# Routed experts' loop: both sets of transposes ahead of the up and down products

## The chip, the core and the metric

The kernel runs on one core of a Trainium2 chip. The metric is the device time of one execution in microseconds (us). Before the change it is 2602.16 us, the median of 3 runs (2601.45 to 2602.78).

## The reference

Two layers of a graph network, each followed by experts. The change touches only the last block, the routed experts (64 experts, 2 per row, 3125 rows of 512 numbers), in which every expert computes, for the rows that were sent to it:

```python
h = silu(buf @ w1[e]) * (buf @ w3[e])     # 512 -> 256
y = h @ w2[e]                             # 256 -> 512
...
return x + shared + routed
```

All of it is float32.

## The kernel before

Stages run one after the other: the attention graph layer, its experts, a normalization, the second graph layer with its gate, and then `phase_moe`, which the profile shows from about 1850 us to the end. In `phase_moe` a first half of the shared expert's products runs beside the routing. Then comes the routed experts' loop (about 1996 to 2446 us), and after it the second half of the shared expert, gathers of the experts' results, and the final sums.

The loop works on items. An item is up to 128 rows of one expert; the trace has 72 of them. Each item needs, by engine:

- POOL gathers its 128 rows (`mo_g`, 256 KB) by an indirect DMA (L2115).
- TensorE (PE) transposes them, four 128x128 blocks (L2218, semaphore `turned`), and ScalarE (ACT) copies the result from PSUM to `mo_xT` (L2265, `cop`).
- PE makes the up products, `mo_xT` by `w13`: 4 calls, 8 instructions of 128x512 in the trace (L2203, `up`).
- ACT takes the sigmoid of one half (L2253, `sgd`), and VectorE (DVE) multiplies twice (L2425, L2427) into `mo_hh` (`hd`).
- PE transposes `mo_hh`, two blocks (L2212, `ht`); ACT copies them to `mo_hT` (L2259, `hc`).
- PE makes the down products, `mo_hT` by `w2`: 2 calls, 4 instructions in the trace (L2225, `yd`); DVE copies the result to `mo_y` (L2433, `yc`); ACT issues the store to `ys` (L2269).
- SP loads each expert's weights four items ahead: `w1` and `w3` (L2063, 512 KB each, into `w13`) when the up products of the item four before are done, and `w2` (L2068, 512 KB) when its down products are. SP issues in order: up load of n, down load of n, up load of n+1.

The items are pipelined by hand. Each engine runs the function `step(n)` in program order; PE's step n works on items n-1 (up), n-2 (transposes of `hh`), n (transposes of the gathered rows) and n-2 again (down). Eight steps are written out, then a loop `Fori` runs bodies of four steps, and the last steps are written out again. No scheduler moves anything: the order in the source is the order on each engine, and only waits on semaphores tie the engines together. The buffers `eX`, `eH`, `eU`, `eY`, `xT`, `sg`, `hh` and `hT` are double.

Of the kernel before, what the change touches and what calls it, by code (L numbers as in the profile page):

```python
# [8 lines left out]
ACT = mybir.ActivationFunctionType  # L9
# [7 lines left out]
P = 128  # L17
N = 3125
D = 512
KT = D // P  # L20
# [19 lines left out]
E1, F1, TOP, CAP1 = 64, 256, 2, 1024  # L40
# [49 lines left out]
def wait(eng, sem, value):  # L90

    if not isinstance(value, int) or value > 0:
        eng.wait_ge(sem, value)
# [1813 lines left out]
FT = F1 // P  # L1907


def phase_moe(nc, K, a, xmid, tab3, xsh, ys, xnT, s13, s2, top, tix, out):  # L1910
# [13 lines left out]
    with Phase(nc, "mo") as p:  # L1924
# [12 lines left out]
        eX, eH, eU, eY = psA, psB, psY, psR  # L1937
# [34 lines left out]
        g = p.sb("g", [P, NW, D])  # L1972
        w2 = p.sb("w2", [P, NW, FT, D])
        xT = p.sb("xT", [P, 2, KT, P])
        sg = p.sb("sg", [P, 2, F1])
        hh = p.sb("hh", [P, 2, F1])
# [34 lines left out]
        turned = p.sem("turned")  # L2011
# [21 lines left out]
        def prev(n, k, q, j):  # L2033

            return n - j, k + (q - j) // NW, (q - j) % NW

        def n_ok(n, q, j):


            if ended[0]:  # L2040
                return q < j
            return not isinstance(n, int) or n >= j
# [111 lines left out]
        @b.tensor  # L2154
        def _(t):
            tens = nc.tensor

            def ranks():
                t.wait_ge(bothd, 1)
                for c in range(CH):  # L2160
                    wait(t, taken, c - 1)
                    cols = both[:, c * TC:(c + 1) * TC, :].rearrange("p t e -> p (t e)")
                    o = (psR, psY)[c % 2]
                    tens.matmul(o[0][:, 0:TC * E1], tri16[:, 0, :], cols, start=True, stop=True)
                    tens.matmul(o[1][:, 0:TC * E1], tri16[:, 1, :], cols, start=True, stop=True).then_inc(ranked, 1)

            def overs():
                t.wait_ge(oqd, 1)
                tens.matmul(psR[1][0:1, 0:P], oq[:], K.ident[:], start=True, stop=True).then_inc(ovd, 1)

            def slots(r):
                t.wait_ge(od, r + 1)
                for i in range(PB):
                    ins = tens.matmul(psR[0][0:NI1, 0:2 * P], oa[:, i, :], ob[:, i, 1:3].rearrange("p w b -> p (w b)"),  # L2174
                                      start=(r == 0 and i == 0), stop=(r == CH - 1 and i == PB - 1), skip_group_check=True)
                ins.then_inc(om, 1)

            def turn():
                t.wait_ge(idd, 1)
                tens.transpose(psR[1][:, 0:NI1], idf[:], K.ident[0:NI1, 0:NI1]).then_inc(idt, 1)  # L2180

            after = {1: ranks, 3: overs, 6: lambda: slots(0), 7: lambda: slots(1), 8: lambda: slots(2),
                     9: lambda: slots(3), 10: lambda: slots(4), 11: turn}
            for j in range(G1):
                for f in range(KT):
                    shared_up(t, j, f)
                    if f == 0 and j:
                        shared_down(t, j - 1)
                    after.get(j * KT + f, lambda: None)()
            shared_down(t, G1 - 1)  # L2190
            t.wait_ge(routed, 1)
            t.wait_ge(zd, NSH)

            def step(n, k, q):
                u = q % 2
                m, km, qm = prev(n, k, q, 1)
                if n_ok(n, q, 1):
                    um = qm % 2
                    t.wait_ge(cop, m + 1)
                    t.wait_ge(wl[qm], km * 32 + 32)  # L2200
                    wait(t, hd, m - 1)
                    for kt in range(KT):
                        ins = tens.matmul(eH[um][:], xT[:, um, kt, :], w13[:, qm, kt, :],  # L2203
                                          start=(kt == 0), stop=(kt == KT - 1))
                    ins.then_inc(up, 1)
                m, km, qm = prev(n, k, q, 2)
                um = qm % 2
                if n_ok(n, q, 2):
                    t.wait_ge(hd, m + 1)
                    wait(t, hc, m - 1)  # L2210
                    for c in range(FT):
                        ins = tens.transpose(eU[um][:, c * P:(c + 1) * P], hh[:, um, c * P:(c + 1) * P], K.ident[:])  # L2212
                    ins.then_inc(ht, 1)
                if n_ok(n, q, 0):
                    t.wait_ge(got[q], k * 16 + 16)
                    wait(t, cop, n - 1)
                    for kt in range(KT):
                        ins = tens.transpose(eX[u][:, kt * P:(kt + 1) * P], g[:, q, kt * P:(kt + 1) * P], K.ident[:])  # L2218
                    ins.then_inc(turned, 1)
                if n_ok(n, q, 2):  # L2220
                    t.wait_ge(hc, m + 1)
                    t.wait_ge(vl[qm], km * 16 + 16)
                    wait(t, yc, m - 1)
                    for c in range(FT):
                        ins = tens.matmul(eY[um][:], hT[:, um, c, :], w2[:, qm, c, :], start=(c == 0), stop=(c == FT - 1))  # L2225
                    ins.then_inc(yd, 1)
            run(t, 2, step)

            for j in range(G1, len(groups)):
                for f in range(KT):  # L2230
                    shared_up(t, j, f)
                    if f == 0 and j > G1:
                        shared_down(t, j - 1)
            shared_down(t, len(groups) - 1)

        @b.scalar
        def _(c_):
# [7 lines left out]
            c_.wait_ge(routed, 1)  # L2245

            def step(n, k, q):
                m, km, qm = prev(n, k, q, 1)
                um = qm % 2
                if n_ok(n, q, 1):  # L2250
                    c_.wait_ge(up, m + 1)

                    nc.scalar.activation(sg[:, um, :], eH[um][:, 0:F1], ACT.Sigmoid).then_inc(sgd, 1)  # L2253
                m, km, qm = prev(n, k, q, 2)
                um = qm % 2
                if n_ok(n, q, 2):
                    c_.wait_ge(ht, m + 1)
                    wait(c_, yd, m - 1)
                    nc.scalar.activation(hT[:, um], eU[um][:, 0:F1].rearrange("p (c t) -> p c t", t=P),  # L2259
                                         ACT.Copy).then_inc(hc, 1)  # L2260
                if n_ok(n, q, 0):
                    u = q % 2
                    c_.wait_ge(turned, n + 1)
                    wait(c_, up, n - 1)
                    nc.scalar.activation(xT[:, u], eX[u][:].rearrange("p (k t) -> p k t", k=KT), ACT.Copy).then_inc(cop, 1)  # L2265
                m, km, qm = prev(n, k, q, 3)
                if n_ok(n, q, 3):
                    c_.wait_ge(yc, m + 1)
                    c_.dma_start(ys[ds(m * P, P), :], y[:, qm, :]).then_inc(st[qm], 16)  # L2269
# [216 lines left out]
```

## Time and profile before

| | |
|---|---|
| median of 3 runs | 2602.16 us |
| the profiled execution's own time | 2601.69 us |
| its span on the core | 2599.8 us |
| PE busy in the span | 2092.5 us (80%) |
| DVE busy | 1466.5 us (56%) |
| POOL busy | 1019.4 us (39%) |
| ACT busy | 658.1 us (25%) |
| mean rate of the DMA engines | 222 GB/s |

A busy share is an average over all stages. What a change in one stage is worth is read from the timeline and the waits of that stage: an engine that is idle for a short time in each turn of a loop pays for it as many times as the loop turns. Matmul durations overlap, so the time that one matmul costs is the distance to the start of the next, and not the duration that its row shows.

### The profile page before, as it was taken

The page shows a single profiled execution, that of the slowest core. Times are in us where ns is not written, and L with a number is a line of the kernel's source. Part 1 is how long each engine was busy: PE and PEld are TensorE (multiplying, and loading weights), DVE is VectorE, ACT ScalarE, POOL GpSimd, SP SyncE. Part 2 cuts the span into 40 slices and gives each one's busy share as a digit, 9 for nine tenths or more (in the row PEclk, how much of TensorE's full clock was granted, in tenths as well). Part 3 has the DMA queues.
Part 4 walks back from the last instruction along what each step waited for, and adds up shares of the span by engine and source line. Part 5 has one row for each costly group of instructions (what it writes and reads, how often), then busy time and mean ns, then how long its engine had stood idle before and what let it go on. Part 6 is the DMA issues. An engine that isn't in the chain of part 4 may idle for free. (4 is left out here: it accounts for less than half of the span.)

```text
span 2599.8 us, 30846 instructions
## 1 busy us (share of the span) xinstructions
PE 2092.5 (80%) x7552; PEld 1232.3 (47%) x7552; DVE 1466.5 (56%) x3483; ACT 658.1 (25%) x2048; POOL 1019.4 (39%) x1082
## 2 busy tenths in 40 slices
PE   3864888888886615339999977789899999999998
PEld 2653666666665614214444422245544444444444
DVE  5447989989998672265554544467673222222243
ACT  1223655655554301320000000034200121212100
POOL 1017777777750003347777777600001111111241
PEclk9887999999997556769999999999799999999999
DMA  5978888888854533687777777686314999999662
GB/s 158 287 286 260 252 250 242 249 239 242 241 165 134 169 97 69 127 278 230 230 233 230 214 210 210 200 293 227 126 46 139 336 340 335 339 338 335 209 232 95
DMA packets 284539, 577.81 MB, mean 222 GB/s; under 512 B 46565, under 2 KB 124613, under 8 KB 281673
## 3 DMA queue, kind: packets, MB, share of 16 engines
q0 software_dynamic: 87136, 303.18, 38.9%
q1 hardware_dynamic: 175827, 234.11, 27.6%
q10 hardware_dynamic: 21462, 39.19, 4.1%
q8 instruction: 47, 0.77, 0.1%
q14 instruction: 67, 0.55, 0.1%
HBM read 476.16 MB, written 101.00 MB: 222 GB/s over the span
## 5 line engine op out<-in xcount | busy, mean ns | idle before, releaser
L801 PE MATMUL g_psA<-g_G,g_oh 128*128 128x261 f32 x1760 | 434.2, 398 | 94.8 <-DVE acc L969 52.3
L1098 PE MATMUL g_psA<-g_G,g_oh 128*128 128x512 f32 x880 | 408.3, 602 | 121.3 <-DVE g_oh L1129 77.2
L1063 POOL DMA_INDIRECT g_G<-tab,src_of_item x440 | 416.6, 947 | 183.7 <-issue 175.5
L741 POOL DMA_INDIRECT g_G<-tab,src_of_item x440 | 419.7, 954 | 157.2 <-issue 104.2
L801 PEld LDWEIGHTS g_psA<-g_G,g_oh 128*128 128x128 f32 x1760 | 328.4, 194 | 165.6 <-DVE g_G L951 97.6
L1098 PEld LDWEIGHTS g_psA<-g_G,g_oh 128*128 128x128 f32 x880 | 159.3, 191 | 348.2 <-issue 339.8
L856 ACT ACTIVATE g_G<-g_G 128x64 f32<-128x64 f32 x1320 | 317.8, 338 | 0.0
L1138 DVE TENSOR_TENSOR acc<-acc,g_psA 128x512 f32 x220 | 151.3, 688 | 282.1 <-PE g_psA L1098 278.8
L2115 POOL DMA_INDIRECT mo_g<-tab,mo_slot x72 | 68.0, 945 | 490.5 <-PE mo_bank L2218 361.4
L2203 PE MATMUL mo_bank<-mo_w,mo_xT 128*128 128x512 f32 x576 | 259.1, 592 | 1.4 <-ACT mo_xT L2265 1.4
L951 DVE TENSOR_TENSOR g_G<-g_G,g_psP 128x640 f32<-128x640 f32 x220 | 179.1, 814 | 5.3 <-ACT g_G L847 5.3
L2139 PE MATMUL mo_bank<-own,s 128*128 128x512 f32 (+1 forms) x448 | 178.1, 556 | 4.3 <-DVE mo_shT L2293 3.1
L2203 PEld LDWEIGHTS mo_bank<-mo_w,mo_xT 128*128 128x128 f32 x576 | 109.3, 190 | 138.7 <-issue 136.8
L969 DVE TENSOR_TENSOR acc<-acc,g_psA 128x522 f32 x220 | 152.6, 693 | 32.0 <-PE g_psA L801 30.7
L2425 DVE TENSOR_TENSOR mo_sg<-mo_sg,mo_bank 128x256 f32<-128x256 f32 x72 | 30.3, 421 | 228.2 <-ACT mo_sg L2253 228.2
L2225 PE MATMUL mo_bank<-mo_w,mo_hT 128*128 128x512 f32 x288 | 142.3, 617 | 11.1 <-ACT mo_hT L2259 6.0
L2139 PEld LDWEIGHTS mo_bank<-own,s 128*128 128x128 f32 x448 | 81.1, 193 | 96.5 <-issue 92.4
L2253 ACT ACTIVATE mo_sg<-mo_bank 128x256 f32<-128x256 f32 x72 | 27.6, 384 | 354.4 <-PE mo_bank L2203 354.4
L1129 DVE TENSOR_SCALAR g_oh<-iota,rel_of_item 128x128 f32<-128x128 f32 x440 | 113.3, 310 | 0.0
L2433 DVE COPY mo_y<-mo_bank 128x512 f32<-128x512 f32 x72 | 49.8, 692 | 108.8 <-PE mo_bank L2225 108.8
L2150 PE MATMUL mo_bank<-s,mo_shT 128*128 128x512 f32 x200 | 89.6, 605 | 9.6 <-DVE mo_shT L2293 3.4
L2130 POOL DMA_INDIRECT own<-ys,mo_pair x50 | 51.0, 1020 | 113.0 <-DVE own L2452 56.5
(382 smaller groups left out, 2635.5 us busy)
## 6 DMA issues: line engine op xcount, KB each, us to landing
mo_w<-in_L_ffn_w SPq DMA_DIRECT2D x216, 512.0 KB, 5.7
ys<-mo_y ACTq DMA_DIRECT2D x72, 256.0 KB, 4.4
fi_rl<-reld POOLq DMA_DIRECT2D x10, 1408.0 KB, 14.5
oht<-fi_oo POOLq DMA_DIRECT2D x10, 1408.0 KB, 10.7
g_G<-tab,src_of_item POOLq DMA_INDIRECT x880, 3.7
g_ot<-oht SPq DMA_DIRECT2D x26, 512.0 KB, 5.5
ys<-sg_zeros SPq DMA_DIRECT2D x24, 512.0 KB, 3.9
g_pen<-pend SPq DMA_DIRECT2D x208, 32.0 KB
```

The source lines that it names most:

```text
L741: q.indirect_dma_start(G[:, j % RING, :], None, tab0, bass.IndirectOffsetOnAxis(K.src[:, j:j + 1], 0)).then_inc(gs[g % 3], 16)
L801: ins = tens.matmul(psA[u][:, f, 0:HW], oh[:, n % OR, h, :], G[:, r + h, f * HW:(f + 1) * HW], start=(h == 0), stop=(h == SUP - 1))
L856: ins = sc.activation(x, x, ACT.Copy, scale=G[:, r, hd * HC + HD:(hd + 1) * HC])
L951: vv.tensor_tensor(x, x, w.unsqueeze(3).to_broadcast([P, SUP, HV, HD]), ALU.mult).then_inc(ready, 1)
L969: vv.tensor_tensor(a1, a1, psA[u][:, :, 0:HW], ALU.add).then_inc(added, 1)
L1063: g.indirect_dma_start(G[:, q, h, :], None, table, bass.IndirectOffsetOnAxis(K.src[:, j:j + 1], 0)).then_inc(got[q], 16)
L1098: ins = nc.tensor.matmul(psA[u][:], oh[:, q % OB, h, :], G[:, q, h, 0:D], start=(h == 0), stop=(h == SUP - 1))
L1129: ins = vv.tensor_scalar(oh[:, q % OB, h, :], K.iota[:], K.rel[:, ds(n * SUP + h, 1)], None, ALU.is_equal)
L1138: ins = vv.tensor_tensor(a1, a1, psA[u][:], ALU.add)
L2139: ins = nc.tensor.matmul(o[c % 2][:, 0:w_], s13[:, i, kt, f * P:(f + 1) * P], xnT[:, tiles[0]:tiles[-1] + 1, kt * P:(kt + 1) * P], start=( ...
L2203: ins = tens.matmul(eH[um][:], xT[:, um, kt, :], w13[:, qm, kt, :], start=(kt == 0), stop=(kt == KT - 1))
L2225: ins = tens.matmul(eY[um][:], hT[:, um, c, :], w2[:, qm, c, :], start=(c == 0), stop=(c == FT - 1))
```

## The change

On PE, step n now begins with the transposes of the gathered rows of item n, then those of `hh` of item n-2; after them the up products of item n-1 and the down products of item n-2. On ACT, the step's order becomes: copy of `xT` for item n, copy of `hT` for item n-2, sigmoid for item n-1, store of item n-3. SP, POOL and DVE keep their programs. No instruction that computes is added or removed, and every wait stands before the same work as before.

```diff
 # PE
             def step(n, k, q):
                 u = q % 2
+                if n_ok(n, q, 0):
+                    t.wait_ge(got[q], k * 16 + 16)
+                    wait(t, cop, n - 1)
+                    for kt in range(KT):
+                        ins = tens.transpose(eX[u][:, kt * P:(kt + 1) * P], g[:, q, kt * P:(kt + 1) * P], K.ident[:])
+                    ins.then_inc(turned, 1)
+                m, km, qm = prev(n, k, q, 2)
+                um = qm % 2
+                if n_ok(n, q, 2):
+                    t.wait_ge(hd, m + 1)
+                    wait(t, hc, m - 1)
+                    for c in range(FT):
+                        ins = tens.transpose(eU[um][:, c * P:(c + 1) * P], hh[:, um, c * P:(c + 1) * P], K.ident[:])
+                    ins.then_inc(ht, 1)
                 m, km, qm = prev(n, k, q, 1)
                 if n_ok(n, q, 1):
...
                 if n_ok(n, q, 2):
-                    t.wait_ge(hd, m + 1)
...
-                    ins.then_inc(ht, 1)
-                if n_ok(n, q, 0):
-                    t.wait_ge(got[q], k * 16 + 16)
...
-                    ins.then_inc(turned, 1)
-                if n_ok(n, q, 2):
                     t.wait_ge(hc, m + 1)
 # ACT
-                if n_ok(n, q, 1):
-                    c_.wait_ge(up, m + 1)
-
-                    nc.scalar.activation(sg[:, um, :], eH[um][:, 0:F1], ACT.Sigmoid).then_inc(sgd, 1)
+                if n_ok(n, q, 0):
+                    u = q % 2
+                    c_.wait_ge(turned, n + 1)
+                    wait(c_, up, n - 1)
+                    nc.scalar.activation(xT[:, u], eX[u][:].rearrange("p (k t) -> p k t", k=KT), ACT.Copy).then_inc(cop, 1)
...
-                if n_ok(n, q, 0):
...
+                if n_ok(n, q, 1):
+                    c_.wait_ge(up, m + 1)
+
+                    nc.scalar.activation(sg[:, um, :], eH[um][:, 0:F1], ACT.Sigmoid).then_inc(sgd, 1)
```

PE, the first of the four steps of the loop's body, before (ISA and REGISTER_ALU rows compute and apply the values of waits; a call of 128x512 is two instructions in the trace):

```order
L2200 ISA
L93 REGISTER_ALU
L2203 MATMUL mo_bank<-mo_w,mo_xT 128x512 x4
L2209 REGISTER_ALU
L93 REGISTER_ALU
L2212 MATMUL mo_bank<-ident,mo_hh 128x128 x2
L2215 ISA
L2218 MATMUL mo_bank<-ident,mo_g 128x128 x4
L2222 ISA
L2225 MATMUL mo_bank<-mo_w,mo_hT 128x512 x2
```

The same step of PE now:

```order
L93 ISA
L2200 MATMUL mo_bank<-ident,mo_g 128x128 x4
L93 REGISTER_ALU
L2208 MATMUL mo_bank<-ident,mo_hh 128x128 x2
L2214 ISA
L93 REGISTER_ALU
L2217 MATMUL mo_bank<-mo_w,mo_xT 128x512 x4
L2224 ISA
L2227 MATMUL mo_bank<-mo_w,mo_hT 128x512 x2
```

The six transposes stood between the up and the down products; they now stand between the down products of one step and the up products of the next. Between the transposes of `hh` and the down products that use them, there were four transposes; there are now the four calls of the up products too.

ACT, the second step of the body, before (the bank is that of the PSUM buffer read):

```order
L2253 ACTIVATE mo_sg<-mo_bank2 128x256
L2259 ACTIVATE mo_hT<-mo_bank5 128x256
L2263 REGISTER_ALU
L2265 ACTIVATE mo_xT<-mo_bank1 128x512
L2269 ISA
L2269 DMA ys<-mo_y 128x512
```

ACT, the same step now:

```order
L2252 REGISTER_ALU
L2254 ACTIVATE mo_xT<-mo_bank1 128x512
L2260 ACTIVATE mo_hT<-mo_bank5 128x256
L2267 ACTIVATE mo_sg<-mo_bank2 128x256
L2271 ISA
L2271 DMA ys<-mo_y 128x512
```

The sigmoid went from the first place to the third, and the copy of `xT` from the third to the first; the store's issue stays last.

## Rows read from the trace of the kernel before

**Rows 1.** Page, section 4: the chain that ended last, by line.

```profile
PE mo_bank L2203 10%; PE mo_bank L2225 5%; PE mo_bank L2139 5%; PE mo_bank L2150 3%; ACT mo_hT L2259 1%; POOL own L2130 1%; DMA own<-ys,mo_pair 0%; PE mo_bank L2174 0%; DVE mo_ssg L2289 0%; DVE mo_shT L2293 0%; PE mo_bank L2212 0%; DVE mo_prd L2354 0%; DVE mo_ovb L2355 0%; DVE mo_pos L2353 0%; DVE mo_prd L2352 0%
```

**Rows 2.** Waits from 2026 to 2436 us: in total, times, longest.

```profile
PEld mo_bank L2225 <- issue: 39.7, 148, 0.5
PEld mo_bank L2225 <- ACT mo_hT L2259: 16.6, 50, 0.3
PE mo_bank L2225 <- ACT mo_hT L2259: 4.8, 16, 0.3
```

**Rows 3.** Timeline, one period: start us, duration us, engine, line, output, inputs, count, [idle].

```profile
2206.65 3.60 PE L2203 MATMUL mo_bank<-mo_w,mo_xT 128*128 128x512 f32 x8
2210.08 0.38 PE L2212 MATMUL mo_bank<-ident,mo_hh 128*128 128x128 f32 x2
2210.28 0.39 ACT L2253 ACTIVATE mo_sg<-mo_bank 128x256 f32<-128x256 f32 x1 [4.91 <-PE mo_bank L2203]
2210.30 0.60 PE L2218 MATMUL mo_bank<-ident,mo_g 128*128 128x128 f32 x4
2210.56 0.38 ACT L2259 ACTIVATE mo_hT<-mo_bank 128x256 f32<-128x256 f32 x1
2210.70 0.42 DVE L2425 TENSOR_TENSOR mo_sg<-mo_sg,mo_bank 128x256 f32<-128x256 f32 x1 [3.06 <-ACT mo_sg L2253]
2210.94 0.60 ACT L2265 ACTIVATE mo_xT<-mo_bank 128x512 f32<-128x512 f32 x1
2210.99 0.30 PEld L2225 LDWEIGHTS mo_bank<-mo_w,mo_hT 128*128 128x128 f32 x2 [0.33 <-ACT mo_hT L2259]
2211.16 0.42 DVE L2427 TENSOR_TENSOR mo_hh<-mo_sg,mo_bank 128x256 f32<-128x256 f32 x1
...
2212.82 3.60 PE L2203 MATMUL mo_bank<-mo_w,mo_xT 128*128 128x512 f32 x8
```

**Rows 4.** The same timeline, the down products of the next step, first of a body.

```profile
2217.37 1.96 PE L2225 MATMUL mo_bank<-mo_w,mo_hT 128*128 128x512 f32 x4 [0.30 <-ACT mo_hT L2259]
```

**Rows 5.** Timeline of PE in the second graph layer's gate stage, straight code.

```profile
1744.81 0.61 PE L1829 MATMUL sg_psT<-ident,sg_ag 128*128 128x128 f32 x4
1745.26 3.60 PE L1836 MATMUL sg_psH<-sg_w,sg_xT 128*128 128x512 f32 x8
1748.69 0.60 PE L1843 MATMUL sg_psN<-ident,sg_xn 128*128 128x128 f32 x4
1749.13 1.00 PE L1819 MATMUL sg_psG<-sg_gT,own 128*128 128x64 f32 x8
```

**Rows 6.** Timeline of PE: up products of item 2, of item 71, and what follows.

```profile
2008.08 3.60 PE L2203 MATMUL mo_bank<-mo_w,mo_xT 128*128 128x512 f32 x8
...
2436.41 3.60 PE L2203 MATMUL mo_bank<-mo_w,mo_xT 128*128 128x512 f32 x8
...
2442.75 0.38 PE L2212 MATMUL mo_bank<-ident,mo_hh 128*128 128x128 f32 x2
```

**Rows 7.** Stretches: length, busy of PE, PEld, DVE, ACT, POOL; PE clock, DMA share, GB/s.

```profile
2000.00:2006.00 6.00, 5.31 (x20) 2.66 (x18) 0.88 (x3) 1.43 (x4) 0.94 (x1) 1.00 1.05 390
2100.00:2200.00 100.00, 97.67 (x290) 46.85 (x290) 24.54 (x48) 20.04 (x48) 15.52 (x17) 1.00 1.00 337
```

**Rows 8.** Page, section 6: DMA issues, count, KB each, us to landing.

```profile
mo_w<-in_L_ffn_w SPq DMA_DIRECT2D x216, 512.0 KB, 5.7
ys<-mo_y ACTq DMA_DIRECT2D x72, 256.0 KB, 4.4
```

**Rows 9.** Timeline of SP: the loads issued after one item's down products.

```profile
2200.68 0.37 SPq L2068 DMA_DIRECT2D mo_w<-in_L_ffn_w  x1
2201.59 0.94 SPq L2063 DMA_DIRECT2D mo_w<-in_L_ffn_w  x2
```

**Rows 10.** Line 2063 from 1990 to 2450 us: issue durations (ns) and landing.

```profile
L2063 SPq DMA_DIRECT2D mo_w<-in_L_ffn_w x136: 372/395/1332, 2000.9 to 2419.9; - x136
...
DMA to landing us min/median/max: 4.3/6.0/9.8
```

More of the change, by code:

```diff
@@ L2207, in step @@
                 um = qm % 2
-                if n_ok(n, q, 2):
-                    t.wait_ge(hd, m + 1)
-                    wait(t, hc, m - 1)
-                    for c in range(FT):
-                        ins = tens.transpose(eU[um][:, c * P:(c + 1) * P], hh[:, um, c * P:(c + 1) * P], K.ident[:])
-                    ins.then_inc(ht, 1)
-                if n_ok(n, q, 0):
-                    t.wait_ge(got[q], k * 16 + 16)
-                    wait(t, cop, n - 1)
-                    for kt in range(KT):
-                        ins = tens.transpose(eX[u][:, kt * P:(kt + 1) * P], g[:, q, kt * P:(kt + 1) * P], K.ident[:])
-                    ins.then_inc(turned, 1)
                 if n_ok(n, q, 2):
@@ L2247, in step @@
             def step(n, k, q):
-                m, km, qm = prev(n, k, q, 1)
-                um = qm % 2
-                if n_ok(n, q, 1):
-                    c_.wait_ge(up, m + 1)
-                    nc.scalar.activation(sg[:, um, :], eH[um][:, 0:F1], ACT.Sigmoid).then_inc(sgd, 1)
+                if n_ok(n, q, 0):
[3 more added lines that the diff above has]
+                    nc.scalar.activation(xT[:, u], eX[u][:].rearrange("p (k t) -> p k t", k=KT), ACT.Copy).then_inc(cop, 1)
                 m, km, qm = prev(n, k, q, 2)
@@ L2260, in step @@
                                          ACT.Copy).then_inc(hc, 1)
-                if n_ok(n, q, 0):
[L2262 to L2265, printed above, removed]
+                m, km, qm = prev(n, k, q, 1)
+                um = qm % 2
+                if n_ok(n, q, 1):
+                    c_.wait_ge(up, m + 1)
+                    nc.scalar.activation(sg[:, um, :], eH[um][:, 0:F1], ACT.Sigmoid).then_inc(sgd, 1)
                 m, km, qm = prev(n, k, q, 3)
```

## The prediction

> **What bounds the kernel now.** I read the chain of waits first: the up products (10% of the span) and the down products (5%) of the routed experts' loop are its two largest pieces, and the copy of `hT` on ACT stands in it with 1% [rows 1]. So TensorE sets the loop's pace, with something small in between. The waits of the loop say what: in 66 steps the down products waited 66 times (50 and 16) for that copy, 21.4 us in all, or 0.32 us each [rows 2]. The timeline of one period shows why: the two transposes of `hh` start at 2210.08, the copy of their result runs from 2210.56 to 2210.94, the four transposes of the gathered rows cover only until about 2210.74 (2210.30 and four distances of 0.11), and the first weight load of the down products comes at 2210.99 [rows 3]. PE is held once in every step by a copy that has only four short transposes to hide behind. In the first step of each loop body the down products start later still, 7.29 us after the mark 2210.08 where the period of 6.17 and the usual 0.91 would make 7.08: some 0.2 us more [rows 3, 4].
>
> **The change, part by part.**
>
> PE's work in a step, without waits: 8 up matmuls take 3.43 us (2206.65 to 2210.08), so 0.43 each, and the 4 down matmuls 1.72. The transposes of `hh` take 0.22 (2210.08 to 2210.30) [rows 3], the other four 0.44, the distance from L1843 to what follows it in the gate stage [rows 5]. Sum: 3.43 + 1.72 + 0.22 + 0.44 = 5.81 us. The loop's real mean is (2436.41 - 2008.08) / 69 = 6.21 us, from item 2's up products to item 71's [rows 6]. The bubble is 0.40 us per step: 0.25 of waiting for ACT, 0.10 for a first weight load that can't start ahead (the up products start at 2212.82, which is 1.83 and not 1.72 after 2210.99) [rows 3], and the 0.2 of one step in four.
>
> *The down products* now have the whole up products between themselves and the transposes they need. The copy of `hT` ends about 0.5 + 0.38 us after those transposes start, behind a copy of `xT` of 0.60 at worst: 1.5 us, against a cover of 3.43 us [rows 3]. The wait goes, and so does the exposed load. In the first step of a body a register computation for the wait on `w2` stood behind the blocked wait for `hT`; nothing blocks there now, so it runs while the up matmuls do. Gain: the whole 0.40.
>
> *What is late next: the transposes of `hh`.* They come first of all that needs the gate, and the up products now queue behind them. The chain to them: up products end at 2210.08, sigmoid at 2210.28, multiplications at 2210.70 and 2211.16, done at 2211.58 [rows 3]: 1.50 us, some 1.55 with the signal. The cover is the down products and four transposes, 1.72 + 0.44 = 2.16 us. A margin of 0.6 us, no wait. ACT has its copies behind it when the sigmoid becomes due (they fall at the step's start), and the store's issue, last on ACT as before, waits for a DVE copy that the down products of the step before released.
>
> *Transposes straight into up products* do not occur in the loop before without a wait. The price lies between 0 and the exposed load of 0.10 per step. The nearest row is the gate stage, the same shapes in the same order with no wait due: four transposes at 1744.81, eight matmuls of 128x512 at 1745.26, 0.45 us where 4 x 0.11 = 0.44 would be [rows 5]. I take 0.01 per step, 1 us in all with what registers add; the end of the range is 0.10, or 6.9 us. I see no reason for a gain below nothing.
>
> *ACT's new order* costs nothing by itself: `xT` is needed a step later (over 5 us for 0.60), `hT` as above. *POOL's gathers* wait for `turned`, still once per step, with four buffers. *SP* is moved past nothing: its loads follow the end of the down and up products at the same places in the step.
>
> *Head.* In the first two steps the up products waited for the copy of `xT` twice; now once, since item 1's copy hides behind item 0's up products. In exchange the first transposes of `hh` wait with no down products as cover: 1.55 - 0.44 = 1.1 us. Saved: 0.9 (0.2 + 0.60 + 0.1 load) and the bubble of 0.35 ahead of item 0's down products. It evens out within 0.2 us; I take 0.
>
> *Tail.* Item 71's up products end at 2439.84 and two transposes at 2440.06, but the next transposes, at 2442.75, put the down products before them at 2442.75 - 1.72 = 2441.03 [rows 6]: a bubble of 1.0 us that goes too. The last item keeps its chain.
>
> Sum: 69 x 0.40 = 27.6, or from the ends 428.3 - 69 x 5.81 = 27.4; + 1.0 tail - 1 for the new transition = 27.4 us. What follows the loop moves with it. The profiled execution took 2601.69 us for a span of 2599.8, so 1.9 lies around it; it becomes 2601.69 - 27.4 = 2574.3. The median of the runs is 0.5 above it: 2574.8, say **2575 us**.
>
> **DMA.** A faster PE asks for more. An item moves three loads of 512 KB, a store of 256 KB [rows 8] and a gather of 128 rows x 512 x 4 bytes: 2.10 MB. In 6.21 us that is 338 GB/s, the 337 of the middle of the loop, at a DMA share of 1.00; in 5.81 us it is 361 GB/s. At the loop's start, with the same kinds of transfer queued, the engines moved 390 GB/s for 6 us [rows 7]. So 361 is within reach, though a share of 1.00 says that not much is left. There is also a store of time: up loads go out at 2201.6 to 2202.5, after the down products that end at about 2200.5 [rows 9], for up products three steps later; 3 x 5.81 + 0.66 - 2.0 = 16 us, less 6.0 to land [rows 10]: 10 us of lead to consume before PE waits at all.
>
> The Trainium skill, in DMA: Bandwidth & Descriptors, section Bandwidth, speaks against this: a load of 1 MB by itself reaches 341 GB/s, and the HBM side is put at about 358 GB/s per core when both of a pair stream. At 341 an item would take 6.15 us and the lead would be gone after some 30 steps: the gain would be 27.4 - (69 x 0.34 - 10) = 14 us, 2588. At 358 it would take 5.86, 3 us in the whole loop, which the lead swallows. The 390 GB/s of the loop's first stretch disagrees with both as a ceiling; the long-run mean here has never been seen above 338.
>
> **Rivals.**
> 1. *DMA becomes the bound.* For it: share 1.00, and issues on SP that last up to 1332 ns instead of 372 [rows 10], as if queues were full. Against it: landing in 6.0 us, under a period, and 390 GB/s. If no more than 338 GB/s can be held, an item takes 6.21: 69 x 0.40 = 27.6 less a lead of 10 is lost, 17.6, so the gain is 10 and the time 2592. If 350 GB/s, the deficit of 0.18 x 69 = 12.6 less 10 costs 3: 2578. It decides below about 352 GB/s. Chance 15%. (The Trainium skill's 341 GB/s, above, would be a case of this one.)
> 2. *The bubble moves instead of going.* The first load of the up products is exposed after the transposes (6.9 us in all) and the register work of the body's first step stays exposed before them (17 x 0.2 = 3.4): 2575 + 9 = 2584. For it: in the loop a load of 0.10 does show. Against it: there it followed a wait; in the gate stage none shows. Chance 12%.
> 3. *Slower: the gate's chain governs.* The transposes of `hh` come before the up products, so a late `hh` now stops all of PE. The chain of 1.55 us has 2.16 of cover; it costs from 2.16 on, and the change loses from 2.16 + 0.40 = 2.56 us. It would take a DVE copy of `y` (0.7 us) plus a store's issue (0.34) both ahead of the gate's work in every step. At 2.7 us the loss is 69 x 0.14 = 10: 2612. The timeline has both well clear of it. Chance 3%.
> 4. *No change*: the wait for `hT` was only the last of several, another 0.3 us behind. The down products' other waits, for `w2` and for `y`, are steps old. Chance 3%.
>
> **How the numbers follow.** Forecast 67%, within 2572 to 2579; rivals 15, 12, 3 and 3%. The range takes in the second rival and most of the first: 2572 to 2588. Faster by over 0.2% (below 2597, about what can be told from no change): 67 + 15 + 12 = 94%, less 1 for what I overlook, 93%. Same 4%, slower 3%.
>
> **What would show it.** In the changed profile, up products should follow each other every 5.81 us, the two transposes of `hh` with no idle before them, the down products with no wait on ACT; the loop's middle should show some 360 GB/s and a clock of 1.00 as now, landing times still near 6 us. Landing times that grow along the loop and waits of PE on DMA in its last third mean rival 1; idle of PEld ahead of the up products means rival 2; idle ahead of the transposes, released by DVE, rival 3.

## The result, and the profile after

The changed kernel takes 2579.44 us (median of 4 runs, 2571.49 to 2585.7); the kernel before, run beside it, 2602.47 (4 runs, 2601.45 to 2608.01). The ratio is 0.9899, 95% interval 0.9876 to 0.9922: 23 us less, where 27 had been forecast. That lies within the stated range of 2572 to 2588 and 0.4 us above the 2572 to 2579 in which the prediction put its own forecast. The profiled execution took 2583.86 us for a span of 2581.8.

The gain is where the prediction put it. Waits of PE (in us, times, longest) from 2012 to 2420 us, in which [rows 2] had 66 waits for the copy of `hT`, 21.4 us in all:

```profile
PEld mo_bank L2217 <- issue: 100.7, 421, 0.2
PEld mo_bank L2227 <- issue: 67.9, 284, 0.2
PEld mo_bank L2200 <- issue: 36.4, 138, 0.3
PEld mo_bank L2208 <- issue: 0.6, 1, 0.6
```

These four are all of PEld's; no row for PE itself and none with ACT, DVE or DMA as releaser is left. The "issue" rows are weight loads that come when their matmul is near, 0.24 us apart from the load before, under a PE that is busy. One period of the timeline (start, duration, engine, line, output, inputs, count, [idle]), to be laid beside [rows 3]:

```profile
2195.01 0.38 PE L2208 MATMUL mo_bank<-ident,mo_hh 128*128 128x128 f32 x2
2195.12 0.30 PEld L2217 LDWEIGHTS mo_bank<-mo_w,mo_xT 128*128 128x128 f32 x2
2195.20 0.60 ACT L2254 ACTIVATE mo_xT<-mo_bank 128x512 f32<-128x512 f32 x1 [1.77 <-PE mo_bank L2200]
2195.22 3.60 PE L2217 MATMUL mo_bank<-mo_w,mo_xT 128*128 128x512 f32 x8
...
2195.70 0.38 ACT L2260 ACTIVATE mo_hT<-mo_bank 128x256 f32<-128x256 f32 x1
...
2198.66 1.88 PE L2227 MATMUL mo_bank<-mo_w,mo_hT 128*128 128x512 f32 x4
...
2198.86 0.38 ACT L2267 ACTIVATE mo_sg<-mo_bank 128x256 f32<-128x256 f32 x1 [2.78 <-PE mo_bank L2217]
...
2199.28 0.42 DVE L2427 TENSOR_TENSOR mo_sg<-mo_sg,mo_bank 128x256 f32<-128x256 f32 x1 [3.81 <-ACT mo_sg L2267]
...
2199.73 0.42 DVE L2429 TENSOR_TENSOR mo_hh<-mo_sg,mo_bank 128x256 f32<-128x256 f32 x1
...
2200.38 0.60 PE L2200 MATMUL mo_bank<-ident,mo_g 128*128 128x128 f32 x4
...
2200.81 0.38 PE L2208 MATMUL mo_bank<-ident,mo_hh 128*128 128x128 f32 x2
```

From 2195.01 to 2200.81 is 5.80 us. The copy of `hT` is done at 2196.08, 2.6 us before the down products at 2198.66. The first weight load of the up products (2195.12) runs beside the transposes of `hh`. `hh` is ready at 2199.73 + 0.42 = 2200.15 and wanted at 2200.81: a margin of 0.66 us. The first weight load of such transposes starts 0.11 us ahead of them (in the step before at 2194.90, for 2195.01), so the room up to that load is 0.55 us.

The ends of the loop, PE's timeline, beside [rows 6]:

```profile
2009.11 0.44 PE L2208 MATMUL mo_bank<-ident,mo_hh 128*128 128x128 f32 x2 [0.95 <-DVE mo_hh L2429]
...
2015.19 3.60 PE L2217 MATMUL mo_bank<-mo_w,mo_xT 128*128 128x512 f32 x8
...
2415.47 3.69 PE L2217 MATMUL mo_bank<-mo_w,mo_xT 128*128 128x512 f32 x8
2418.99 1.88 PE L2227 MATMUL mo_bank<-mo_w,mo_hT 128*128 128x512 f32 x4
...
2421.57 1.98 PE L2227 MATMUL mo_bank<-mo_w,mo_hT 128*128 128x512 f32 x4 [0.47 <-ACT mo_hT L2260]
```

Item 2's up products start at 2015.19 and item 71's at 2415.47: 400.3 us, against 428.3 before. The loop's middle, from 2100 to 2200 us (length, busy time of PE, PEld, DVE, ACT, POOL, then PE clock, DMA share, GB/s), answers to [rows 7]:

```profile
2100.00:2200.00 100.00, 100.00 (x311) 49.66 (x310) 26.76 (x53) 21.71 (x52) 16.06 (x17) 1.00 1.04 361
```

PE is busy for all of it at full clock. The DMA engines move 361 GB/s, and this has a price, hidden so far: the page's DMA issues (count, KB each, us to landing; compare [rows 8]), and line 2063 from 1990 to 2420 us (compare [rows 10]):

```profile
mo_w<-in_L_ffn_w SPq DMA_DIRECT2D x216, 512.0 KB, 7.9
ys<-mo_y ACTq DMA_DIRECT2D x72, 256.0 KB, 5.7
```

```profile
DMA to landing us min/median/max: 4.6/7.0/12.8
```

**Where the whole time went.** I split each trace in three: up to the first transposes of gathered rows, from there to the start of the last down matmul (the loop), and the rest. The two ends are in the rows of the two lines (duration ns min/median/max, first and last start), first of the kernel before, then of after:

```profile
L2218 PE MATMUL mo_bank<-ident,mo_g x288: 272/273/323, 1995.6 to 2434.2; 128*128 128x128 f32 x144
L2225 PE MATMUL mo_bank<-mo_w,mo_hT x288: 592/592/697, 2006.3 to 2445.0; 128*128 128x512 f32 x144
```

```profile
L2200 PE MATMUL mo_bank<-ident,mo_g x288: 272/273/323, 2002.7 to 2409.8; 128*128 128x128 f32 x144
L2227 PE MATMUL mo_bank<-mo_w,mo_hT x288: 592/592/697, 2012.8 to 2423.0; 128*128 128x512 f32 x144
```

| us | ahead of the loop | loop | behind it |
|---|---|---|---|
| before | 1995.6 | 449.4 | 154.8 |
| after | 2002.7 | 420.3 | 158.8 |
| difference | +7.1 | -29.1 | +4.0 |

The loop gained 29.1 us, and 11.1 came back in stages whose code is the same. Most of the 7.1 arises at the end of the first graph layer, where this execution was granted less clock: the same DVE instruction starts 0.6 us later than before at 724 us and 9.4 us later at 823, and other stages then bring this to 10.6 and back to 7.1. Before, then after (same columns):

```profile
750.00:800.00 50.00, 40.23 (x195) 31.27 (x195) 46.01 (x108) 26.65 (x113) 6.84 (x8) 0.97 0.19 52
```

```profile
750.00:800.00 50.00, 42.76 (x184) 33.22 (x183) 41.59 (x98) 23.94 (x100) 7.64 (x8) 0.86 0.20 57
```

Of the 4.0 behind the loop, 3.0 lie in one group of 16 matmuls of the shared expert; before, then after:

```profile
2495.41 7.10 PE L2150 MATMUL mo_bank<-s,mo_shT 128*128 128x512 f32 x16 [3.30 <-DVE own L2452]
```

```profile
2474.38 10.12 PE L2150 MATMUL mo_bank<-s,mo_shT 128*128 128x512 f32 x16 [3.24 <-DVE own L2454]
```

This too is clock. TensorE had its full clock (2.4 GHz) in this group before, and half of it (1.2 GHz) for the first part of the group after:

```profile
2495.00:2499.00 4.00, 3.59 (x9) 1.71 (x10) 2.45 (x4) 0.00 (x0) 3.09 (x4) 1.00 1.02 386
```

```profile
2474.00:2478.00 4.00, 3.62 (x5) 1.59 (x6) 2.48 (x4) 0.00 (x0) 3.08 (x4) 0.50 1.03 406
```

Before, PE stood idle for 3.30 us ahead of this group and not ahead of the 16 matmuls before it; after, for 1.71 us ahead of those and for 3.24 us ahead of this one.

### The profile page after: what moved, and what is told of

The parts are those of the page before. It is cut to its first block and busy times, and to the rows that moved or that the text cites. A ratio compares the mean times of both kernels' runs of the same rounds, so it can differ in the third digit from the quotient of the medians.

```text
span 2581.8 us, 30782 instructions
## 1 busy us (share of the span) xinstructions
PE 2086.6 (81%) x7552; PEld 1238.7 (48%) x7552; DVE 1464.1 (57%) x3483; ACT 658.3 (25%) x2048; POOL 1019.2 (39%) x1082
## 5 line engine op out<-in xcount | busy, mean ns | idle before, releaser
L801 PE MATMUL g_psA<-g_G,g_oh 128*128 128x261 f32 x1760 | 443.9, 405 | 93.0 <-DVE acc L969 50.5
L801 PEld LDWEIGHTS g_psA<-g_G,g_oh 128*128 128x128 f32 x1760 | 335.2, 198 | 165.9 <-DVE g_G L951 95.5
L1098 PEld LDWEIGHTS g_psA<-g_G,g_oh 128*128 128x128 f32 x880 | 159.3, 191 | 349.4 <-issue 343.7
L2217 PEld LDWEIGHTS mo_bank<-mo_w,mo_xT 128*128 128x128 f32 x576 | 103.8, 190 | 103.8 <-issue 103.3
L2227 PE MATMUL mo_bank<-mo_w,mo_hT 128*128 128x512 f32 x288 | 135.4, 592 | 0.5 <-ACT mo_hT L2260 0.5
L2150 PE MATMUL mo_bank<-s,mo_shT 128*128 128x512 f32 x200 | 92.6, 621 | 11.3 <-DVE mo_shT L2295 5.1
L1085 ACT ACTIVATE g_xrT<-g_psU 128x512 f32<-128x512 f32 x25 | 14.9, 597 | 316.5 <-PE g_psU L1107 316.5
L943 DVE TENSOR_TENSOR g_oh<-iota,rel_of_item 128x256 f32<-128x256 f32 x220 | 91.2, 415 | 1.1
## 6 DMA issues: line engine op xcount, KB each, us to landing
oht<-fi_oo POOLq DMA_DIRECT2D x10, 1408.0 KB, 10.6
```

Source lines behind the costliest of these rows:

```text
L801: ins = tens.matmul(psA[u][:, f, 0:HW], oh[:, n % OR, h, :], G[:, r + h, f * HW:(f + 1) * HW], start=(h == 0), stop=(h == SUP - 1))
L1098: ins = nc.tensor.matmul(psA[u][:], oh[:, q % OB, h, :], G[:, q, h, 0:D], start=(h == 0), stop=(h == SUP - 1))
L2150: ins = nc.tensor.matmul(psY[n % 2][:], shT[:, (j * KT + f) % HR, i * P:(i + 1) * P], s2[:, f, :], start=(f == 0), stop=(f == KT - 1))
```

## The experiments

All experiments ran on chips on which the stages ahead of the loop take some 220 to 270 us longer (the kernel before: 2846 to 2869 us). The changed kernel's loop in its traces there is the same to 0.1 us, so I compare loop lengths as defined above, mean steps (from one start of the up products to the next), and ratios to the kernel before, run beside each. The kernel before was not traced there. Variants without a ratio ran once; for them I read the trace alone. Results first:

| | loop us | step us | ratio to before |
|---|---|---|---|
| changed kernel (e1, e11) | 420.3, 420.3 | 5.81 | 0.9910, 0.9899 |
| e2 PE's order alone | 495.0 | 6.82 to 6.99 | |
| e3 ACT's order alone | 511.0 | 7.03 to 7.27 | |
| e4 `hh` first, gathered rows after up | 420.8 | 5.81 | 0.9909 |
| e5 old order, longer cover | 454.5 | 6.27 | 0.9993 |
| e6 one more DVE operation | 421.3 | 5.81 | |
| e7 two more | 435.0 | 5.92 to 6.08 | |
| e8 half of the up products | 374.3 | 5.21 | |
| e9 up products turned | 412.6 | 5.73 | 0.9883 |
| e10 e4's order, one more DVE operation | 421.5 | 5.81 | |
| e12 least cover, one more DVE operation | 439.3 | 6.02 to 6.12 | |

**The changed kernel again (e1, e11).** No edit.

> The changed kernel once more, to see how much of its scatter lies in the loop. Theory (the bubble of 0.40 us per step is gone, all else is unchanged): the loop turns in 5.81 us per item in every run, the ratio to the kernel before is 0.989 to 0.991 (about 2577 us), and the stages ahead of the loop and behind it differ from profile to profile by several us in both directions. Rival (the change also makes the stage behind the loop or the stages ahead of it slower, by code that lies elsewhere or by another start time): the loop again 5.81 us, but the stages ahead again some 7 us and the stage behind again some 4 us longer than in the kernel before.

> The changed kernel again, on the same chip as the turned version, to compare the two. Theory: loop 420.3 us as in its two profiles, ratio to the kernel before 0.99; the stages around the loop differ by some us from profile to profile, in no fixed direction. Rival: the stage behind the loop again 3 to 4 us longer than the 154.8 us of the kernel before.

The ratios are 0.991 (0.9877 to 0.9943) and 0.9899 (0.9847 to 0.9951). 29.1 us of 2848 would be 0.9898. The loop is 420.3 us both times and 157.8 and 163.1 us stand behind it. Read against the 154.8 of the kernel before, that is 3.0 and 8.3 us more, so taken by its letter the rival is not refuted. But all the variants have 157.8 to 166.0 there, and those that keep PE's old order (e3 with 163.7, e5 with 165.9) no less than the others. In e3 and e5 the same group of 16 matmuls takes 9.86 us and starts at a clock of 0.50, after PE had been idle for 9.1 and 10.9 us. So the stretch behind the loop gets longer with the old order too; what sets the clock there is not shown, and one trace of the kernel before, with its 154.8, is little to compare with.

**One half of the change alone (e2, e3).** e2 is the changed kernel with ACT's order of before, e3 the kernel before with ACT's new order:

```diff
 # e2, ACT's step
-  xT(n); hT(n-2); sigmoid(n-1); store(n-3)
+  sigmoid(n-1); hT(n-2); xT(n); store(n-3)
 # e3, ACT's step
-  sigmoid(n-1); hT(n-2); xT(n); store(n-3)
+  xT(n); hT(n-2); sigmoid(n-1); store(n-3)
```

> PE in the new order, ACT in the old (sigmoid, copy of hT, copy of xT). Theory (copies have to stand ahead of the sigmoid, since they would otherwise wait for the up products): the copy of hT starts only after the sigmoid that follows the up products, 0.20 + 0.38 + 0.38 + 0.05 us after they end, and the first load shows 0.10: 1.1 us of bubble per item, 6.9 us per item, about 2602 + 69 x 0.7 = 2652 us. Rival (PE's order alone carries the gain, ACT's is a by-product): 5.81 us per item, about 2577 us.

> ACT in the new order, PE in the old. Theory: the copy of hT stands behind the copy of xT, 0.98 us later than before, and the down products wait for it: 7.2 us per item, 2602 + 69 x 0.98 = 2670 us. Rival (ACT's order alone carries the gain): 6.0 us per item or less, under 2595 us.

Both are slower than either whole kernel, by about what was expected: the loop is 46 us longer than before in e2 (48 expected, 69 x 0.7) and 62 in e3 (68 expected). e2's timeline:

```profile
2450.56 0.38 ACT L2255 ACTIVATE mo_sg<-mo_bank 128x256 f32<-128x256 f32 x1 [5.84 <-PE mo_bank L2217]
2450.84 0.38 ACT L2261 ACTIVATE mo_hT<-mo_bank 128x256 f32<-128x256 f32 x1
...
2451.27 0.30 PEld L2227 LDWEIGHTS mo_bank<-mo_w,mo_hT 128*128 128x128 f32 x2 [1.58 <-ACT mo_hT L2261]
```

The copy of `hT` has its transposes long before, but stands behind a sigmoid that waits for the up products; so the up products that should cover the copy delay it instead. In e3 the copy stands behind that of `xT`, which waits for the last of the six transposes:

```profile
2456.24 0.60 ACT L2252 ACTIVATE mo_xT<-mo_bank 128x512 f32<-128x512 f32 x1 [5.89 <-PE mo_bank L2218]
...
2456.73 0.38 ACT L2258 ACTIVATE mo_hT<-mo_bank 128x256 f32<-128x256 f32 x1
...
2457.16 1.13 PE L2225 MATMUL mo_bank<-mo_w,mo_hT 128*128 128x512 f32 x2 [0.96 <-ACT mo_hT L2258]
```

The change works only as a pair: against the changed kernel, PE's half alone costs 75 us and ACT's half 91.

**Which transposes go first (e4).** PE: transposes of `hh`, up products, transposes of the gathered rows, down products; ACT: `hT`, sigmoid, `xT`.

> PE: transposes of hh, up products, transposes of the gathered rows, down products; ACT: hT, sigmoid, xT. The chain from the up products through the gate to the transposes of hh is 1.55 us and has only the down products as cover, 1.72 us instead of 2.16. Theory (what counts is that each chain is shorter than its cover): no wait, 5.81 to 5.83 us per item, the same time as the changed kernel within 2 us, less a slower head of at most 1 us. Rival (signals and loads take more than the timeline shows, so a margin of 0.17 us isn't enough): 5.9 us per item or more, 6 us or more slower than the changed kernel.

The same: 420.8 us, step 5.81, ratio 0.9909 (0.9872 to 0.9946). What counts is that the up products lie between the transposes of `hh` and the down products; that *both* sets of transposes come first counts for nothing. I had misread this order's other cover, though: see e10.

**Only the cover, in the old order (e5).** The kernel before, whose four transposes of the gathered rows are made twice:

```diff
-                    for kt in range(KT):
+                    for kt in range(2 * KT):
+                        kt = kt % KT
                         ins = tens.transpose(eX[u][:, ...
```

> The kernel before with the four transposes of the gathered rows done twice in every step: 0.44 us more work for PE, and as much more cover for the copy of hT. Theory (of the bubble of 0.40 us, 0.25 is the wait for the copy, 0.10 is a weight load that shows only because of the wait, 0.05 the register work of one step in four that is behind the wait): the wait falls under its cover, so an item takes 5.81 + 0.44 = 6.25 us, the time is 3 us above the kernel before, 2605 us. Rival (the load of the down products shows after every set of transposes, wait or not): 6.35 us per item, 2612 us. If the bubble was work and not a wait: 6.65 us, 2632 us.

As expected: 6.24 us a step, 6.35 in the first of a body. PE's work is 5.81 + 0.44 = 6.25, so the wait *and* the exposed first load of 0.10 us per step are gone with 0.44 us more cover, and from 2300 to 2640 us no row of PE's waits names ACT. Its down products follow at once:

```profile
2449.98 1.04 PE L2219 MATMUL mo_bank<-ident,mo_g 128*128 128x128 f32 x8
...
2450.74 0.30 PEld L2226 LDWEIGHTS mo_bank<-mo_w,mo_hT 128*128 128x128 f32 x2
...
2450.85 1.88 PE L2226 MATMUL mo_bank<-mo_w,mo_hT 128*128 128x512 f32 x4
```

0.44 us of extra work per item makes a step 0.06 us longer on average (6.27 against 6.21), so it bought back 0.38 us of the bubble's 0.40; ratio 0.9993 (0.9954 to 1.0033). This shows that all but 0.02 to 0.03 us of the bubble was a lack of cover. The 0.10 us that stay in one step of four are what is left of the body's first step.

**How much the gate's chain may grow (e6, e7, e10, e12).** One or two more multiplications on DVE ahead of the gate's two, into a buffer that nobody reads:

```diff
                     cv = Chain(v, vch, m)
+                    for i in range(1):                 # e7: range(2)
+                        vv.tensor_tensor(late[:, i], sg[:, um, :], eH[um][:, 0:F1], ALU.mult)
```

> The changed kernel with one more multiplication of 128x256 on DVE ahead of the gate's two, written to a buffer that nobody reads: the gate's chain grows by 0.45 us, its margin before the transposes of hh is 0.61 to 0.66 us. Theory: no wait, 5.81 us per item, unchanged within the scatter. Rival (the loop is now held by DMA or by the gate's chain and only looks like PE): for the gate's chain 69 x 0.45 = 31 us slower.

> The same with two more multiplications: the chain grows by 0.9 us. Theory (margin 0.66 us): 0.24 us of wait in each item, 6.05 us, with a first load of 0.05 to 0.10 us more that shows behind it, 6.1 us; 69 x 0.27 = 19 us slower than the changed kernel, about 2597 us. Rival (the transposes may slip behind other work on PE, or DMA sets the pace at 361 GB/s): unchanged, 5.81 us.

e6 costs nothing per step (5.81); its 1.0 us (421.3) lies in the loop's first and last steps. e7 costs 14.7 us in the loop where 19 were expected, since an added operation costs less than the 0.45 us between the gate's own two. Those two depend on each other; the added ones don't:

```profile
2449.94 0.75 DVE L2429 TENSOR_TENSOR mo_late<-mo_sg,mo_bank 128x256 f32<-128x256 f32 x2 [3.78 <-ACT mo_sg L2268]
2450.61 0.42 DVE L2430 TENSOR_TENSOR mo_sg<-mo_sg,mo_bank 128x256 f32<-128x256 f32 x1
...
2455.37 1.88 PE L2228 MATMUL mo_bank<-mo_w,mo_hT 128*128 128x512 f32 x4
...
2457.67 0.20 PEld L2209 LDWEIGHTS mo_bank<-ident,mo_hh 128*128 128x128 f32 x2 [0.22 <-DVE mo_hh L2432]
```

Two take 0.67 us (2449.94 to 2450.61). That is no more than the margin of 0.66 up to the transposes, but more than the 0.55 up to their first load. The last two rows show the wait, in the next step: the load comes 2.30 us after the down products start (2455.37 to 2457.67), and would stand 2.16 - 0.11 = 2.05 after without a wait; the transposes start with it, 0.14 us late, and take 0.29 us instead of 0.21.

e10 puts one such operation into e4's order, where I thought that the down products alone, 1.72 us, cover the chain.

> The order hh, up, gathered rows, down with one more multiplication of 128x256 on DVE in the gate's chain. One such costs 0.33 us when it stands back to back with the next. With the transposes of the gathered rows behind the up products the cover is 1.72 us instead of 2.16. Theory (a chain that is longer than its cover costs the difference): margin 0.15 - 0.33 = -0.18, so 0.18 to 0.28 us of wait per item, 6.0 to 6.1 us, the loop 13 to 19 us longer than 420.8; the same multiplication cost the changed kernel nothing in its loop. Rival (the cover of the gate's chain is not what the order sets): 5.81 us again.

The theory's number fell: 5.81 us, no loss. The mistake was mine and lies in the order: with transposes of `hh`, up, gathered rows, down, the four transposes of the gathered rows still stand behind the up products, so the cover is 1.72 + 0.44 = 2.16 us as in the changed kernel, and the chain of 1.55 + 0.33 = 1.88 fits. e12 makes the test that e10 was meant to be, with the order `hh`, gathered rows, up, down:

> The changed kernel with the transposes of hh put ahead of those of the gathered rows (and on ACT the copy of hT ahead of that of xT), and one more multiplication of 128x256 on DVE ahead of the gate's two, into a buffer that nobody reads. Now only the down products stand between the end of the up products and the transposes of hh: a cover of 1.72 us. By the theory (PE waits where the chain from the up products to hh, 1.55 + 0.33 us, is longer than the cover) each item waits 0.16 us, and 0.3 with a first load that is exposed after a wait: a step of 5.97 to 6.1 us, the loop from first gathered-row transposes to last down products 432 to 441 us instead of 420.3. The rival, that the margin seen in the changed kernel isn't set by the down products and the four transposes, but that PE has slack elsewhere, gives 5.81 and 421 us.

Its loop takes 439.3 us and a step 6.02 to 6.12. PEld's waits from 2300 to 2640 us, and one step:

```profile
PEld mo_bank L2203 <- DVE mo_hh L2432: 35.9, 42, 0.9
```

```profile
2453.28 1.88 PE L2228 MATMUL mo_bank<-mo_w,mo_hT 128*128 128x512 f32 x4
...
2454.68 0.42 DVE L2432 TENSOR_TENSOR mo_hh<-mo_sg,mo_bank 128x256 f32<-128x256 f32 x1
2455.16 0.20 PEld L2203 LDWEIGHTS mo_bank<-ident,mo_hh 128*128 128x128 f32 x2 [0.82 <-DVE mo_hh L2432]
2455.16 0.44 PE L2203 MATMUL mo_bank<-ident,mo_hh 128*128 128x128 f32 x2
...
2455.43 0.60 PE L2209 MATMUL mo_bank<-ident,mo_g 128*128 128x128 f32 x4
```

The chain from 2453.28 to 2455.16 is 1.88 us against a cover of 1.72; the transposes also take 0.27 instead of 0.22 us, because their first load can't run ahead. So the same added operation that is free behind 2.16 us of cover (e6, e10) costs 18 us behind 1.72 (e12's 439.3 against e6's 421.3). The order of e12 was not run without the added operation; that it would then cost nothing is my estimate, from the chain of 1.55 against 1.72. By it, the changed kernel's order of the two sets of transposes is a reserve, not a gain.

**How far the DMA engines are from their limit (e8).** Half of the up products are left out (the result is then that of half the inputs' columns), all loads stay:

```diff
-                    for kt in range(KT):
+                    for kt in range(KT // 2):
                         ins = tens.matmul(eH[um][:], xT[:, um, kt, :], w13[:, qm, kt, :],
```

> The changed kernel with only the first two of the four up products of each item (half of the 512 inputs are left out of the sum): PE needs 4.09 us per item instead of 5.81, and all transfers stay. It measures how fast the DMA engines can feed the loop. Theory (361 GB/s is not the ceiling; the first 6 us of the loop before ran at 390): DMA takes over at 380 to 400 GB/s, 5.25 to 5.5 us per item, 2550 to 2560 us. Rival (the changed loop already stands at the ceiling of DMA, share 1.04): about 361 GB/s, 5.8 us per item, about 2577 us. If DMA was no bound at all: 4.1 us per item.

PE's work would be 5.81 - 1.72 = 4.09 us; a step takes 5.21, and PE now waits for the weights. The wait (as above, from 2300 to 2640 us) and the middle of the loop (columns as above):

```profile
PE mo_bank L2217 <- DMA mo_w<-in_L_ffn_w: 30.7, 33, 1.2
```

```profile
2400.00:2500.00 100.00, 82.13 (x267) 40.79 (x266) 28.93 (x57) 23.73 (x57) 17.95 (x19) 1.00 1.07 397
```

33 of the 65 waits name these loads. The other 32 name the copy of `xT` for a later item, or nothing; with the rate at 397 GB/s in each 100 us from 2300 to 2600 I take them for waits on the same loads, which the rows alone don't show. So the limit of these transfers, fed like this, is 397 GB/s, or 2.10 MB / 397 = 5.3 us per item. The changed kernel at 361 stands 9% below it.

**A version without the transposes of `hh` (e9).** The up products are computed turned, with the weights as the stationary operand, 32 matmuls of 128 columns, so that `mo_hh` is what `hT` was; its transposes and copy fall away:

```diff
-                    for kt in range(KT):
-                        ins = tens.matmul(eH[um][:], xT[:, um, kt, :], w13[:, qm, kt, :],
-                                          start=(kt == 0), stop=(kt == KT - 1))
+                    for c in range(2 * FT):
+                        for kt in range(KT):
+                            ins = tens.matmul(eH[um][:, c * P:(c + 1) * P], w13[:, qm, kt, c * P:(c + 1) * P],
+                                              xT[:, um, kt, :], start=(kt == 0), stop=(kt == KT - 1))
```

> A version meant to beat both: the up products are computed turned round (the weights are the operand that is loaded, the rows' transposes the one that streams: 16 calls with 128 columns for 4 with 512), so their result has the layout that the down products load, and both transposes of hh and the copy of hT go. Theory (an item costs what PE's columns cost, and no chain is longer than its cover): 0.22 us less per item, 3.43 + 1.72 + 0.44 = 5.59 us, the loop some 17 us shorter than the changed kernel's 420 us, ratio to the kernel before about 0.983; DMA has to deliver 375 GB/s, under the 397 that the run with half of the up products reached. Rival 1 (weight loads of 128 columns don't hide behind matmuls of 128 columns): 0.12 us or more for each of 32 matmuls instead of 0.107, 6.0 us per item, slower than the changed kernel by 14 us. Rival 2 (DMA sets the pace between 361 and 375 GB/s once lead is used up): 5.65 to 5.75 us per item in the last third of the loop.

The loop is 7.7 us shorter than the changed kernel's, not 17. The 0.22 us of transposes go, but the up products take longer:

```profile
2453.74 3.65 PEld L2210 LDWEIGHTS mo_bank<-mo_xT,mo_w 128*128 128x128 f32 x32
2453.85 3.74 PE L2210 MATMUL mo_bank<-mo_xT,mo_w 128*128 128x128 f32 x32
...
2457.42 1.88 PE L2220 MATMUL mo_bank<-mo_w,mo_hh 128*128 128x512 f32 x4
```

2453.85 to 2457.42 is 3.57 us, 0.112 per matmul, instead of 3.43. The weight loads fill that time themselves (3.65 us for 32, end to end). The first rival was right in kind, and its 0.12 us per matmul too high. The ratio, 0.9883 (0.9825 to 0.9942), can't be told from e11's 0.9899 of the same series: its loop is shorter in the trace, a shorter total isn't shown.

## Why the prediction was right, point by point

**The bubble** (0.40 us per step, 27.4 to 27.6 in all): right. From item 2's up products to item 71's the loop gained 428.3 - 400.3 = 28.0 us. Of that, 0.44 is only moved to the head: item 3's transposes now stand ahead of item 2's up products. That leaves 27.6. All three parts went: the wait, the exposed load (e5 shows that it existed only because of the wait) and the body's first step. e5's steps show 0.38 of the 0.40 to be missing cover. For the last part the prediction's cause, register work behind a blocked wait, isn't shown on its own: in e5, without a blocked wait, half of it (0.10 us) stayed, in the changed kernel nothing.

**The new transition**, transposes straight into up products, was put at 0.01 us per step, 1 us in all, with 0.10 as the far end: it costs nothing. Transposes of `hh` at 2195.01 and up products at 2195.22 are 0.21 apart. The gate stage [rows 5] was the right row to take.

**Head**: from the first transposes to item 2's up products it is 12.4 us before (1995.65 to 2008.08) and 12.5 after (2002.69 to 2015.19). That stretch now also holds item 3's transposes (0.44) and those of item 1's `hh` (0.22), so 0.6 us were gained where the forecast was 0 within 0.2. The step that was mis-sized: item 1's transposes now stand ahead of item 0's up products too, and cover part of the copy that those wait for (PE waits 0.25 us there, where it was 0.69). The wait of 0.95 us in the head came as forecast (1.1).

**Tail**: from item 71's up products to the start of the last down matmul it is 8.6 us before and 7.5 after; 0.22 of this are the transposes of item 70's `hh`, which now stand ahead of item 71's up products, 0.9 the bubble, forecast 1.0.

Sum for the loop: 27.6 + 0.6 + 0.9 = 29.1, forecast 27.4. Of the difference, 1 us is the transition and the rest the head, with rounding.

**The gate's chain** as the next thing to be late: right in size. Forecast a margin of 0.6 us, measured 0.66, or 0.55 up to the transposes' first load, which the prediction didn't count; e6, e7 and e12 bracket it: 0.33 us more is free, 0.67 makes PE wait, and 0.33 more with 0.44 less cover costs 18 us.

**DMA**: the forecast that 361 GB/s is within reach was right, and its first rival therefore wrong: no wait on DMA stands in the loop, and e8 puts the limit at 397. The 390 GB/s of [rows 7] was a fair witness. The Trainium skill, in DMA: Bandwidth & Descriptors, section Bandwidth, gives 341 GB/s for a lone 1 MB load and 425 for one of 16 MB, and says that for transfers from HBM the side at about 358 binds, a figure that it ties to both cores of a pair streaming. With one core at work, 361 for the whole loop and 397 in e8 lie above 341 and 358, and the measurement decides: e8's queued loads of 512 KB went more like its 16 MB load than like its 1 MB one. No run here has the pair's other core at work, so none tests the 358 in its own case.

One expectation failed: landing times were to stay near 6 us. The median of line 2063 went to 7.0 and the longest from 9.8 to 12.8. For line 2068 the median went from 5.1 to 8.1, and it grew along the loop's first part: 7.1 from 2012 to 2140 us, 8.2 and 8.4 in the two stretches of 140 us behind it. The prediction called landing times that grow, with waits of PE on DMA, a sign of its first rival; they grew, then stayed, at a rate of 359 to 363 GB/s from 2100 to 2400 us, and PE never waited. The prediction's lead of 10 us was also taken from a median over all loads of line 2063, while the up products need the later load of each pair. One pair before (issued at 2201.59, [rows 9], and 2202.06), and one after (issued at 2195.68 and 2196.15):

```profile
DMA to landing us min/median/max: 5.5/6.7/7.8
```

```profile
DMA to landing us min/median/max: 6.3/8.9/11.6
```

Before, the later one lands at 2209.9, 9.3 us ahead of the up products at 2219.16. After, it lands at 2207.7, 4.9 us ahead of those at 2195.22 + 3 x 5.81 = 2212.65. Over the loop (without its first 18 and last two items) this lead was 9.3 to 11.3 us before and is 4.0 to 6.9 now. Half of the store of time is gone: queues were not costed as getting longer with the rate, and should have been.

**The total.** The forecast for the profiled execution was 2574.3, its time 2583.86. The loop came out 1.7 us better, and 11.1 us were lost ahead and behind. The prediction said that what follows the loop moves with it and took no scatter of other stages into the sum. The median of four runs is 2579.44, within the range, 4 us above the value. How near it came is in part luck: single runs lie from 3.5 us below the value to 11 above, and the mechanism rests on the loop's 29.1 us, not on this median. The changed kernel's four runs span 14 us, those of before 6.6. On the experiments' chips both spread by tens of us (2806 to 2839 changed, 2826 to 2867 before, in e1's series), so I don't read a wider spread into the change. Whether the loop's earlier end does something to the clock granted after it is open, since no run changes that alone; that e3 and e5 with their later ends show the same drop speaks against it.

## What to carry to other kernels

In a software pipeline written by hand, ask of each producer and consumer pair which work lies between them, and put the longest block between the pair with the longest round trip through another engine; then check the round trip that lost that cover. Move the same step on every engine that it passes through: with either half of this change alone the loop is 46 to 62 us longer than without any. A shorter step raises the rate of transfers, so look at how long before its use the last transfer of each set lands, not only at the rate or at a median.

## What the runs showed of the hardware that I had not expected

- The first weight load of a group of 128x512 matmuls showed as 0.10 us only where the group had waited for another engine; with the wait gone it ran under the previous group, at transposes into products as well (2195.12 under 2195.01), and in e5 too.
- Two independent DVE multiplications of 128x256 in a row cost 0.33 us each, although each row shows 0.42; the gate's two dependent ones are 0.45 apart.
- The DMA engines held 397 GB/s over 100 us with one core's 512 KB loads, 256 KB stores and gathers, at a share of 1.07. At 361 GB/s a 512 KB load of line 2068 landed after 8.1 us in the median, at 338 after 5.1.
- 32 matmuls of 128 columns, each with its own weight load, take 3.57 us; the same product as 8 instructions of 512 columns takes 3.43.
